# Two-block decoder on one core: first attention's masks and maxima as 64-row matmuls, last attention's transposed scores as 64x64 tiles, and a new order of all pieces

## The reference

```
x = x + L0_attn(ln(x))         # 16 heads of 16, causal; q, k, v, o projections with ternary weights and
                               # activations rounded to 8 bit per token
x = x + L0_xattn(ln(x), ctx)   # WKV recurrence over the positions, v = ctx
x = x + L0_ffn(ln(x))          # (sigmoid(x w1) * (x w2)) w3, ternary weights, 704 hidden
x = x + L1_attn(ln(x))         # 32 query heads of 8, 8 key heads, rotary positions, no mask
x = x + L1_xattn(ln(x), ctx)   # 32 heads of 8; keys of ctx (window 64) and of x (window 32) side by side, alibi
x = x + L1_ffn(ln(x))          # dense layer + shared and top-2-of-6 routed rank-16 experts
```

## Time and profile before

| | us |
|---|---|
| median of 3 runs (lowest, highest) | 776.13 (775.43, 779.71) |
| the profiled execution | 773.48 |
| its span, first to last instruction | 771.7 |
| PE busy in the span | 645.9 (84%) |
| DVE busy | 572.1 (74%) |
| ACT busy | 507.1 (66%) |
| POOL busy | 297.1 (39%) |
| mean granted TensorE clock, share of 2.4 GHz | 0.974 |

### The profile page before, as it was taken

The page is one execution under the profiler, slowest core; times in us unless marked ns, Lnnn a source line. Parts: engine busy times, 40 slices in busy tenths (PEclk is TensorE's granted clock), DMA queues, the critical chain, the costliest instruction groups (busy, mean ns, idle before and its releaser), DMA issues. The chain is left out here.

```text
span 771.7 us, 19045 instructions
## 1 busy us (share of the span) xinstructions
PE 645.9 (84%) x6669; PEld 359.8 (47%) x6692; DVE 572.1 (74%) x1632; ACT 507.1 (66%) x1229; POOL 297.1 (39%) x472
## 2 busy tenths in 40 slices
PE   1598998865668779889999986799999999998885
PEld 0255555543446557645445433344444444445553
DVE  5588886679999997678778754567676666666786
ACT  3588888587768766468887763366666766665421
POOL 2215543176679988665556302111211211101110
PEclk9999999988789999999999999999999999999999
DMA  4676775311111101155434514335335434330101
GB/s 161 141 163 125 162 176 67 60 35 58 36 44 37 35 21 35 36 90 83 73 71 77 84 34 91 61 56 87 68 56 88 69 72 79 53 46 11 35 28 42
DMA packets 162303, 54.90 MB, mean 71 GB/s; under 512 B 148448, under 2 KB 160160, under 8 KB 161952
## 3 DMA queue, kind: packets, MB, share of 16 engines
q1 hardware_dynamic: 162208, 53.68, 35.4%
HBM read 16.69 MB, written 5.24 MB: 28 GB/s over the span
## 5 line engine op out<-in xcount | busy, mean ns | idle before, releaser
L1163 DVE TENSOR_REDUCE l1x_neg_max<-bank 128x2 f16<-128x448 f32 (+1 forms) x192 | 119.6, 641 | 47.6 <-PE bank L1270 44.8
L1218 ACT ACTIVATE l1x_probs<-bank 128x512 f32<-128x512 f32 x192 | 106.4, 595 | 54.6 <-PE bank L1291 40.5
L871 DVE TENSOR_REDUCE l1a_neg_max<-bank 128x4 f16<-128x512 f32 x128 | 83.5, 684 | 32.7 <-PE bank L959 32.0
L1115 POOL TENSOR_TENSOR q_stack<-l1x_q_sum,q_stack 128x512 f16<-128x512 f32 x16 | 18.5, 1157 | 183.8 <-ACT q_stack L1210 183.8
L919 ACT ACTIVATE l1a_probs<-bank 128x512 f32<-128x512 f32 x128 | 69.5, 595 | 27.6 <-PE bank L973 27.0
L1662 PE MATMUL bank<-mix_xT_parts,w_ternary 128*128 128x256 f16 x384 | 50.0, 283 | 6.1 <-DVE mix_hidden L1544 4.0
L558 DVE TENSOR_REDUCE l_neg_max<-bank 128x4 f16<-128x512 f32 x64 | 42.3, 683 | 13.6 <-PE bank L685 13.6
L1662 PEld LDWEIGHTS bank<-mix_xT_parts,w_ternary 128*128 128x128 f16 x384 | 37.8, 102 | 15.3 <-DVE mix_hidden L1544 6.4
L1475 POOL TENSOR_TENSOR mix_hidden_parts<-mix_hidden,mix_hidden_parts 128x256 f16<-128x256 f32 x48 | 38.0, 804 | 15.1 <-ACT mix_hidden_parts L1607 15.1
L631 ACT ACTIVATE l_probs<-bank 128x512 f32<-128x512 f32 x64 | 36.6, 599 | 10.7 <-PE bank L705 10.7
L1734 POOL TENSOR_TENSOR moe_rstd<-moe_var_eps,minus_half 128x1 f32<-128x1 f32 x16 | 8.8, 550 | 75.2 <-DVE moe_var_eps L1752 75.2
(11 more groups left out here) (265 smaller groups left out, 1787.9 us busy)
## 6 DMA issues: line engine op xcount, KB each, us to landing
ctx_projected<-mix_ctx_projected SPq DMA_DIRECT2D x16, 192.0 KB, 1.9
l1x_ctx_projected<-ctx_projected SPq DMA_DIRECT2D x16, 160.0 KB, 2.4
x_residual<-x_in SPq DMA_DIRECT2D x4, 512.0 KB, 5.0
mix_ctx_in<-ctx_in SPq DMA_DIRECT2D x16, 128.0 KB, 2.3
out_dram<-moe_out SPq DMA_DIRECT2D x16, 128.0 KB, 1.7
w_f<-w_in SPq DMA_DIRECT2D x2, 704.0 KB, 6.2
w_attn_f<-w_l_in SPq DMA_DIRECT2D x1, 1024.0 KB, 6.8
q_stack<-q_begin_in SPq DMA_DIRECT2D x1, 1024.0 KB, 5.4
```

What stands on the lines that cost most here:

```text
L871: dve.tensor_reduce(mm[:, 16 * j + 4 * s:16 * j + 4 * s + 4], b_s[c % 3][:].rearrange("p (r k) -> p r k", k=P), AX.X, ALU.max, negate=True ...
L1163: dve.tensor_reduce(mm[:, first:first + count], scores, AX.X, ALU.max, negate=True).then_inc(s_max, 1)
L1218: act.activation(prob[:, c, :], b_st[c % 2][:], ACT.Exp).then_inc(s_exp, 1)
```

## The change

- **l0 masks.** `cmask` holds, twice over in rows 0 to 63 and 64 to 127, two 64x64 triangles and four 64x128 placement matrices. A mask is now four matmuls with 64 rows: for each half z of the keys or queries, one per bank, 256 columns each. The constant's load is 128 x 640 floats where it was 128 x 256, and it is cast by one DVE instruction instead of two.
- **l0 row maxima.** DVE writes them so that the transposed maxima of a half's heads lie in that half's 64 rows; ACT copies all 128 rows; the 8 matmuls that add them have 64 rows and alternate between the halves.
- **l1x transposed scores.** Each matmul of an ST piece becomes two of 64x64, so a piece has 12 matmuls where it had 6.
- **Order.** Every row of `ORDERS` and `TIMES` is new; `PACE` has one pace for each quarter of a stage, and `clock` adds them up. The number of pieces and their depth in the pipelines are as before. The diff shows two rows of `ORDERS` and one entry of `TIMES`.

```
     ("l0", "act"): order("""
-        F5+2 OE-2 ST.2-1 ST.3-1 F3+3 F8a.0+2 F8a.1+2 T3d-3 M T3e-3 F3e+3 T4-3 ST.0 F3f+3 F8v+2 ST.1"""),
+        T4-6 F8v-1 F3f ST.0-3 ST.1-3 F5 F3+1 OE-4 ST.2-3 ST.3-3 F8a.0 T3d-5 T3e-5 F8a.1 F3e+1 M-2"""),
     ("l0", "pe"): order("""
-        T4-3 S.0+1 T5-3 F5+3 T1-2 ST.1 S.1+1 F7+3 PV M+1 ST.0+1"""),
+        T4-6 M-3 ST.0-3 T5-6 S.0-2 F5 T1-5 ST.1-3 F7 S.1-2 PV-3"""),
...
-    masks = arena.tile("masks_f32", [P, 2, P], F32)
+    masks = arena.tile("masks_f32", [P, 640], F32)
...
-        for dst, heads, m in ((net.cmask[:, 0], 4, 0), (net.cmask[:, 1], 4, 1)):
-            ins = dve.tensor_copy(dst.rearrange("p (h k) -> p h k", k=P), masks[:, m].unsqueeze(1).to_broadcast([P, heads, P]))
-        chained(ins)
+        chained(dve.tensor_copy(net.cmask[:], masks[:]))
...
-PACE = {"l0": (0, 8, 8.0, 11.73), "mix": (150.0, 1.35, 15.88, 5.97), "l1a": (263.0, 1.53, 8.18, 15.58), "l1x": (441.5, 6.93, 13.05, 26.37), "moe": (677.0, 5.96, 4.55, 4)}
+PACE = {"l0": (0, 12.468, (11.783, 1.218, 6.511, 13.874), 11.336),
+        "mix": (144.28, 1.424, (16.729, 13.518, 10.517, 11.112), 8.575),
+        "l1a": (246.11, 3.398, (9.0, 8.648, 4.565, 19.784), 12.382),
+        "l1x": (435.15, 8.562, (16.274, 15.338, 13.08, 12.595), 25.814),
+        "moe": (694.41, 2.589, (3.802, 4.347, 3.706, 12.932), 2.414)}
-    ("l0", "sp"): (2.445,),
...
+    ("l0", "sp"): (0.498,),
...
 def clock(stage, n, turn):
 
-    start, fill, pace, drain = PACE[stage]
-    return start + fill * min(turn - 1, 0) + pace * min(max(turn - 1, 0), n - 1) + drain * max(turn - n, 0)
+    start, fill, paces, drain = PACE[stage]
+    part = (n - 1) / len(paces)
+    run = sum(pace * min(max(turn - 1 - k * part, 0), part) for k, pace in enumerate(paces))
+    return start + fill * min(turn - 1, 0) + run + drain * max(turn - n, 0)
 
...
-    mt = sb("neg_maxT", [NH, P], F16)
+    mt = sb("neg_maxT", [P, P], F16)
+    halves = slice(0, 64), slice(64, P)
+    triangle = [net.cmask[:, 64 * m:64 * m + 64] for m in range(2)]
+    placed = [[net.cmask[:, P * (1 + 2 * m + z):P * (2 + 2 * m + z)] for z in range(2)] for m in range(2)]
...
-                dve.tensor_reduce(mm[:, 4 * c:4 * c + 4], b_s[c % 2][:].rearrange("p (h k) -> p h k", k=P),
+                dve.tensor_reduce(mm[:, 64 * (c % 2) + 4 * (c // 2):64 * (c % 2) + 4 * (c // 2) + 4], b_s[c % 2][:].rearrange("p (h k) -> p h k", k=P),
...
-                act.copy(mt[:], b_s[0][0:NH, 0:64].bitcast(F16)).then_inc(s_mt, 1)
+                act.copy(mt[:], b_s[0][:, 0:64].bitcast(F16)).then_inc(s_mt, 1)
...
-                for j in range(2):
-                    pe.matmul(b_s[j][:], net.identb[:], net.cmask[:, 0, :], start=True, stop=False, skip_group_check=True)
+                for z in range(2):
+                    for j in range(2):
+                        pe.matmul(b_s[j][:].rearrange("p (h z n) -> p h z n", h=4, z=2)[:, :, z, :], placed[0][z][halves[j], :],
+                                  triangle[0][halves[j], :].unsqueeze(1).to_broadcast([64, 4, 64]), start=z == 0, stop=False,
+                                  skip_group_check=True)
...
-                for j in range(2):
-                    pe.matmul(b_st[j][:], net.identb[:], net.cmask[:, 1, :], start=True, stop=False, skip_group_check=True)
+                for z in range(2):
+                    for j in range(2):
+                        pe.matmul(b_st[j][:].rearrange("p (h z n) -> p h z n", h=4, z=2)[:, :, z, :], placed[1][z][halves[j], :],
+                                  triangle[1][halves[j], :].unsqueeze(1).to_broadcast([64, 4, 64]), start=z == 0, stop=False,
+                                  skip_group_check=True)
...
-                for j in range(2):
-                    for x in range(4):
-                        h = 8 * c + 4 * j + x
-                        ins = pe.matmul(b_st[j][:, P * x:P * x + P], net.ident16[0:NH, h:h + 1].to_broadcast([NH, P]), mt[:],
-                                        start=False, stop=x == 3, skip_group_check=True)
+                for x in range(4):
+                    for j in range(2):
+                        row = 64 * j + 4 * c + x
+                        ins = pe.matmul(b_st[j][:, P * x:P * x + P], net.ident16[halves[j], row:row + 1].to_broadcast([64, P]),
+                                        mt[halves[j], :], start=False, stop=x == 3, skip_group_check=True)
...
-                tiles = [(b_st[j], slice(64 * j, 64 * j + 64)) for j in range(2)]
+                tiles = [(b_st[j][64 * u:64 * u + 64, :], slice(64 * j, 64 * j + 64), slice(64 * u, 64 * u + 64))
+                         for u in range(2) for j in range(2)]
                 if c % 3 < 2:
                     s = 2 * (c // 3) + c % 3
                     for z in range(2):
-                        for ps, rows in tiles:
-                            pe.matmul(ps[:].rearrange("p (r z q) -> p r z q", r=4, z=2)[:, :, z, :], net.xkm[rows, z, :],
+                        for ps, rows, keys in tiles:
+                            pe.matmul(ps.rearrange("p (r z q) -> p r z q", r=4, z=2)[:, :, z, :], net.xkm[rows, z, keys],
                                       net.identr[rows, 0:256].rearrange("p (r q) -> p r q", r=4), start=z == 0, stop=False,
                                       skip_group_check=True)
-                    for ps, rows in tiles:
-                        ins = pe.matmul(ps[:], kt[rows, b % 3, s, 0:2, :].rearrange("p x k -> p (x k)"),
+                    for ps, rows, keys in tiles:
+                        ins = pe.matmul(ps, kt[rows, b % 3, s, 0:2, :].rearrange("p x k -> p (x k)")[:, keys],
                                         qt[rows, b % 3, 4 * s:4 * s + 4, :].rearrange("p r q -> p (r q)"),
                                         start=False, stop=True, skip_group_check=True)
                 else:
-                    for ps, rows in tiles:
-                        pe.matmul(ps[:], net.xkm[rows, 2, :], net.identr[rows, :], start=True, stop=False,
+                    for ps, rows, keys in tiles:
+                        pe.matmul(ps, net.xkm[rows, 2, keys], net.identr[rows, :], start=True, stop=False,
                                   skip_group_check=True)
                     for x in range(2):
                         s = 2 * (c // 3) + x
-                        for ps, rows in tiles:
-                            ins = pe.matmul(ps[:, 256 * x:256 * x + 256], kt[rows, b % 3, s, 2:4, :].rearrange("p x k -> p (x k)"),
+                        for ps, rows, keys in tiles:
+                            ins = pe.matmul(ps[:, 256 * x:256 * x + 256], kt[rows, b % 3, s, 2:4, :].rearrange("p x k -> p (x k)")[:, keys],
                                             qt[rows, b % 3, 4 * s:4 * s + 4, 64:P], start=False, stop=True,
                                             skip_group_check=True)
                 ins.then_inc(s_st, 1)
@@ -1869,7 +1882,7 @@
         sb("stage_memory", [P, (EVEN + ODD) // 4])
         net.X = sb("x_residual", [P, NB * C])
...
-        net.cmask = sb("causal_masks", [P, 2, 512], BF16)
+        net.cmask = sb("causal_masks", [P, 640], BF16)
...
-    cmask = np.where(t[None, :] <= t[:, None], np.float32(0), masked)
+    h = np.arange(64)
+    triangle = np.where(h[None, :] <= h[:, None], np.float32(0), masked)
+    after, before = triangle.copy(), triangle.T.copy()
+    after[63], before[0] = masked, masked
+    placed = np.zeros((2, 2, 64, P), np.float32)
+    for z in range(2):
+        for i in range(64):
+            placed[0, z, i, 64 * z + i] = i < 63
+            placed[1, z, i, 64 * z + i] = i > 0
...
-    masks = np.stack([cmask, cmask.T], 1)
+    masks = np.concatenate([after, before] + [placed[m, z] for m in range(2) for z in range(2)], 1)
+    masks = np.concatenate([masks, masks], 0)
```

88 lines of the change are left out of this document (44 added, 44 removed), and 38 rows, old and new, of the table TIMES.

## The result

| us | before | after |
|---|---|---|
| median (lowest, highest), 4 runs each | 775.78 (774.02, 779.71) | 730.58 (728.74, 734.63) |
| ratio, 95% interval | | 0.942 [0.937, 0.947] |
| the profiled execution, its span | 773.48, 771.7 | 734.63, 732.8 |
| PE busy, DVE, ACT | 645.9, 572.1, 507.1 | 620.9, 573.9, 499.7 |
| mean granted clock | 0.974 | 0.963 |

The profiled execution of the changed kernel was the slowest of its four.

A forecast was written before the change was run, and what follows sets the result against it. Bounds: a PE-DVE-ACT loop in l0, DVE in mix, PE in l1x, dependent chains at joints. -12.6 - 7.3 - 1.5 - 4 = -25.4 us from 773.48 gives 748.1, plus 2.65 to the median: 750.7 us, range 733 to 771.

The forecast's parts named there:

- the joints' term: Between stages: starting l1x and mix one item earlier removes PE's 2.72 us DMA wait and 1.3 us at l0/mix, -4 us.
- Rival B: At the joints: the new order recovers 20 us of PE's 31 idle us instead of 4, 734.7 us; chance 0.12.
- l0, -12.6: First attention block: narrower matmuls and new order cut an item from 8.19 to 7.35 us over 15 steps, -12.6 us.
- the loop of the forecast: In an l0 item: a chain through PE, DVE and ACT, put at 7.0 us after the change, level with ACT's 7.02.
- l1x tiles, -7.3: Last attention: 64x64 transposed scores remove five changes of matmul form per item at 0.10 us each, -7.3 us.
- A (l0 keeps 8 us): In l0: moved pieces eat the matmul gain, items end at 8.0 us, joints give nothing, 764.3 us; chance 0.18.
- C (doubled matmuls cost): In l1x's ST pieces: the 6 more matmuls each cost 24 ns, +13.8 us, giving 764.5 us; chance 0.07.
- E (the change of form still costs): In l1x and l1a: the drain is not tied to tile shape, so -7.3 and -1.5 fall away, 759.5 us; chance 0.05.
- D (mix starves DVE): In mix: six hidden tiles per pair each make in-order DVE wait 0.8 us, +34 us, giving 785 us; chance 0.08.
- l1a's -1.5: In l1a: four S/ST neighbours of one form per item instead of three, 15 x 0.10, -1.5 us.
- mix's 0: Mix stage: same work, DVE-bound, depth unchanged, so no change in time, 0 us.
- the -1.3 of their joint: Between l0 and mix: mix also starts an item earlier, counted as 1.3 us of the -4 us for joints.

The follow-up runs named there:

- mm_new_tail: mm_old_order with the changed kernel's rows, times and paces for l1a, l1x and moe, all three starting 17 clock units later than there: 736.18 us.
- mm_l1x_turn_3_58: New matmuls, old rows for l0, mix and l1a, new rows and paces for l1x and moe, l1x starting 3.58 l1a turns after l1a's last item's turn: 744.32 us.
- mm_old_order: The changed kernel with the order and pace tables of the kernel before, so both matmul changes under the old order: 755.85 us, ratio 0.978.
- mm_l0_rows_new: mm_old_order with only l0's rows of ORDERS and TIMES replaced by the new ones: 755.77 us, ratio 0.976.
- changed_again: The changed kernel run once more without any edit: 729.00 us, ratio 0.941.

## Why the prediction was wrong

**Direction and most costs held; the step that failed is the joints' term.** "I take the first of these and 1.3 us more from the same at the l0/mix joint: -4 us." Measured: -11.5 at the joint from l1a to l1x and -4.3 between the PVs of items 14 and 15 (a joint too, l1x to moe, which the text did not name). What l0 to mix gave is not known apart; it lies in the stretch up to the last l1a S, which is 4 us shorter on average. Over three executions of the changed kernel the first is -6.8, -11.5 and -11.9, the second -4.3 or -4.4. In the profile of the result that is -15.8 where -4 stood, 12 of the 13.5 us by which the profiled executions miss the sum (38.9 against 25.4); the start's 2.3 us, which I had priced at 0, is most of the rest, and I did not trace it. I priced one wait, the 2.72 us of the earlier trace rows, where the row of the stretch, 40.09 busy of 55 us, named 15 us of idle time and a clock of 0.94. That one wait fell from 2.7 to 1.8 us; the other 8 us of idle time were in waits that I had not priced, and 2.5 us of busy time went with the lower clock. Rival B (the joints close, 734.7) was the right mechanism with a chance of 0.12; its counter-argument, "the order around them is much the same", was read from PE's list alone and is what mm_new_tail against mm_l1x_turn_3_58 refutes: l1a's rows and l1x's place had changed together, and together they took the joint from 54.0 to 44.7 us.

**l0, -12.6.** Measured -11.9, and -12.0 in mm_old_order. The prices of the pieces were right (0.23 us; 0.77 against 0.79). Two reasons for it were not, so that the number was met in part by luck. First, F7's place and the joined exponentials were counted as part of the change's effect in l0; mm_l0_rows_new shows that the rows give nothing beside the matmuls with the loads as they stand. Second, "ACT's own work, 7.02 us per item, is the floor": ACT's busy time is not fixed. It is 67.37 of 74 us for items of 7.26 us, 6.6 us each; two exponentials side by side take 1.10 us where two apart take 0.60 and 0.61. The order is not all of it: in mm_old_order, over ten items (60.0 to 132.6 us), it is 68.22 us, 6.8 each; I take it that closer items leave fewer instructions standing alone. What ends the item in the changed kernel is, in part, the transposing DMA, which the loop of the forecast did not have in it. ACT is busy for 91% of the middle of l0 (over 93 forecast) and PE for 86 (75 forecast). PE's busy time per item fell by 1.25 us in mm_old_order (107.92 to 89.12 over 15), not 1.8, although the starts of the groups give the full 1.8; I did not find out where the rest is counted.

**l1x tiles, -7.3.** As PE work right: -5.9 in the old order, -7.0 in the new one, against 6.9 for 14 items. As time 4.1 and some 3.7. The mis-sized part is what the text took as covered by "PE is 96% busy": the remaining 4% are waits for ACT's exponentials, and they grow as PE gets faster (6.6 to 8.4 us). In the new order they are nearly gone (0.8 us in l1x), and others stand there, again a transposing DMA:

```profile
PE bank L1275 <- DMA l1x_kT<-k_stack: 4.5, 5, 1.5
PE bank L1275 <- DVE l1x_neg_max L1175: 3.5, 16, 0.3
PE bank L1300 <- ACT l1x_probs L1230: 0.8, 3, 0.3
```

The new order gave l1x 4.4 us of its own (194.6 to 190.2), which I had not counted at all.

**Rivals.** A (l0 keeps 8 us) is refuted by an item of 7.26 us. C (doubled matmuls cost) is refuted: eight masks in 0.22 us. The rule behind it, by the Trainium skill's TensorEngine Tiling (Array Packing), Restrictions, is that column tiling switches the fast weight load off; the 106 ns of a narrow load agree with it, but the loads have cover, so it set no time. E (the change of form still costs) is refuted by 0.29 to 0.19 us. D (mix starves DVE) has its mechanism in the trace, at a ninth of its price of 34 us: DVE's waits for POOL's hidden parts went from 3.5 us (150 to 345 us before) to 7.4 (136 to 331 us after):

```profile
DVE mix_hidden L1557 <- POOL mix_hidden_parts L1488: 7.4, 5, 2.3
```

Mix is hardly longer for it: from its first to its last output 84.9 us before, and 85.6, 79.8 and 82.8 in three executions of the changed kernel. l1a's -1.5, mix's 0 and the -1.3 of their joint lie in one stretch. It fell by 1.4 in the profile of the result, but it took 295.8, 290.9 and 293.5 us in three executions of the changed kernel; on average over all profiles it fell by 4.0 where 2.8 stood, and no run sets the three terms apart. That the medians differ by 45.2 us and the profiled executions by 38.9 comes from which executions were profiled: before, one 2.3 us under its median, after, one 4.05 us over it.

## What to carry to other kernels

Price a joint between stages by all of its idle time and its granted clock, not by its longest wait: here the longest wait was 2.7 us, and 9.0 us of idle time and 2.5 us of busy time at the lower clock went. Test orders by whole neighbourhoods: changes to one stage gave nothing three times (l0's rows, l1x's rows, moe's start), l1x's and moe's rows and paces together gave 11.5 us, and three stages together 20. When a bound engine gets faster, first look at the small waits it still has, since part of the gain goes there; and when transposing DMAs are in a loop, try not to put two big loads behind one another on the engine that issues them: that gain, 3 us, is likely and not certain.

## What the runs showed of the hardware

- **A change of tile form** on TensorE cost 0.10 us: eight 64x64 matmuls of 224 columns take 0.29 us ahead of a 64x128 group and 0.19 ahead of a 64x64 one.
- **The clock** fell to 1.2 GHz in the middle of a busy kernel (changed_again), behind a stretch in which PE had been busy for 1.75 of 4 us, and stayed up at the same place in two other executions of the same kernel; the joint with the fall was 5 us longer. The Trainium skill (TensorE: Matmul & The Clock Gate, HAM oscillation) has waits for a DMA start the work behind them at the lower clock. The trace of mm_old_order agrees, with 0.55 from 460 to 463 us and 0.50 from 463 to 468, behind the 2.71 us wait that ended at 459.94; the kernel before does not, with 1.00 for 5 us behind its 2.72 us wait.
- **A busy time is no floor.** ACT's busy time per item went from 7.02 us (70.20 for ten items) to 6.6, with the same instructions. Two that stand side by side took less than two apart: 1.10 us against 0.60 and 0.61.
- **A transposing DMA behind big loads.** Right behind loads of 1.8 MB, issued on SP too, the issue of the second transpose took 3.66 us where it mostly takes 1.3.
